# First attention of a fused two-layer kernel: q and k spread to head rows by DMA through DRAM

## The reference

```
h = ln(x); q, k, v = split(h @ w_qkv + b_qkv)            # 16 heads of 8 channels
scores = q @ k.T / sqrt(8)     # a bucket of 64 tokens sees itself (causal) and the bucket before
x1 = x + (softmax(scores) @ v) @ w_out + b_out
```

## Time and profile before

| | |
|---|---|
| time, median of 3 runs | 1061.87 us (1061.46 to 1066.82) |
| profiled execution, span | 1062.5 us |
| busy in the span: PE, DVE, ACT, POOL | 944.1, 859.6, 756.3, 405.7 us |
| granted TensorE clock, mean | 0.950 |
| first scores product of the first attention | 17.07 us |
| first instruction of the next stage | 244.5 us |

### The profile page before, as it was taken

How to read it: one execution, slowest core, us unless ns; L and a number is a source line. 1 busy time by engine, 2 the same in 40 slices (tenths; PEclk the granted TensorE clock), 3 DMA queues, 4 the chain that set the end, 5 groups by cost and what they waited for, 6 DMA issues and landing times. The chain is left out here.

```text
span 1062.5 us, 28952 instructions
## 1 busy us (share of the span) xinstructions
PE 944.1 (89%) x10222; PEld 607.5 (57%) x10222; DVE 859.6 (81%) x2328; ACT 756.3 (71%) x1476; POOL 405.7 (38%) x568
## 2 busy tenths in 40 slices
PE   5999999994889999999999999678888874899996
PEld 3788888872445444444444444246666653788862
DVE  4988988845888999868899999848888866888854
ACT  2666666645889888888888878346767653688854
POOL 3544444443354100000000000023478867676653
PEclk9999999967899999999999999969999985999998
DMA  8333333000002200032212222010111102232318
GB/s 268 123 107 107 107 106 108 24 3 20 1 6 74 72 1 1 1 104 70 77 71 75 87 66 74 20 53 22 32 52 51 54 27 74 75 86 82 85 45 221
DMA packets 61005, 72.60 MB, mean 68 GB/s; under 512 B 8875, under 2 KB 37805, under 8 KB 60865
## 3 DMA queue, kind: packets, MB, share of 16 engines
q1 hardware_dynamic: 50080, 59.36, 17.9%
q0 software_dynamic: 4544, 8.60, 2.4%
q10 hardware_dynamic: 6240, 2.79, 1.1%
HBM read 40.14 MB, written 31.49 MB: 67 GB/s over the span
## 5 line engine op out<-in xcount | busy, mean ns | idle before, releaser
L808 ACT ACTIVATE d__hf<-d__HB,dense__d 128x512 f32<-128x512 f32 x288 | 184.7, 679 | 39.2 <-PE d__HB L1047 38.2
L867 DVE TENSOR_TENSOR d__hl<-d__hf,d__hh 128x1024 f16<-128x1024 f32 x144 | 173.6, 1219 | 20.4 <-ACT d__hh L813 18.1
L813 ACT ACTIVATE d__hh<-d__hf 128x1024 f16<-128x1024 f32 x144 | 152.2, 1057 | 4.6
L781 POOL TENSOR_SCALAR d__rstd<-d__mv 128x4 f32<-128x4 f32 x16 | 14.2, 886 | 353.6 <-DVE d__mv L990 353.6
L1045 PE MATMUL d__YB<-d__hh,d__w2h 128*128 128x512 f16 x288 | 110.5, 384 | 2.5 <-DVE d__tmp L924 2.5
L1046 PE MATMUL d__HB<-d__xl,d__w1h 128*128 128x512 f16 x288 | 110.9, 385 | 0.0
L1045 PE MATMUL d__HB<-d__xh,d__w1h 128*128 128x512 f16 x288 | 110.8, 385 | 0.0
L1047 PE MATMUL d__HB<-d__xh,d__w1l 128*128 128x512 f16 x288 | 110.6, 384 | 0.0
L316 POOL TENSOR_SCALAR_AFFINE_SELECT a__pt<-a__pt 128x512 f32<-128x512 f32 x128 | 81.3, 657 | 75.4 <-ACT a__pt L364 75.3
L1046 PE MATMUL d__YB<-d__hl,d__w2h 128*128 128x512 f16 x288 | 110.1, 382 | 0.0
L1047 PE MATMUL d__YB<-d__hh,d__w2l 128*128 128x512 f16 x288 | 109.9, 382 | 0.0
(11 more groups left out here) (402 smaller groups left out, 2544.4 us busy)
## 6 DMA issues: line engine op xcount, KB each, us to landing
rows<-a__blank SPq DMA_DIRECT2D x72, 268.0 KB, 3.2
d__G<-gates SPq DMA_DIRECT2D x64, 256.0 KB, 3.2
c__xin<-rows SPq DMA_DIRECT2D x39, 134.0 KB, 2.2
dense__stage<-e_w SPq DMA_DIRECT2D x16, 256.0 KB, 3.1
b__stage<-e_w SPq DMA_DIRECT2D x32, 128.0 KB, 2.2
c__yb<-parts SPq DMA_DIRECT2D x8, 256.0 KB, 8.4
c__yb<-parts ACTq DMA_DIRECT2D x8, 256.0 KB, 8.9
out<-c__xo SPq DMA_DIRECT2D x8, 256.0 KB, 2.3
```

What stands on the lines that cost most here:

```text
L808: act.activation(hf[:, q, f], HB[:, f], gelu, scale=1.0 / WS, bias=b1[:, at:at + 1]).then_inc(s_["h_free"], 1)
L813: act.activation(hh[:, j % (LEAD + 1), f - 1:f + 1], hf[:, q, f - 1:f + 1], ACT.Copy).then_inc(s_["hi_done"], 1)
L867: dve.tensor_tensor(hl[:, p, f], hf[:, q, f], hh[:, p, f], ALU.subtract).then_inc(s_["lo%d_done" % i], 1)
```

## The change

The spread products, their evictions and the constant `spread` are gone. In their place SP writes `high` and `low` of a batch to a small DRAM buffer `spill` and, when each write has landed, reads them back six times with rows placed four apart: channel d of a head goes to rows 4d + r for r = 0, 1, 2, and the maxima's rows are now 3 and 7 (mod 32). `high` and `low` have two buffers. The rows of `qs` and `ks` that no read writes are set once at the start (VectorE: five memsets, and constants_of() behind stats(0), which also splits b_out in three). Normalising moves to ScalarE (activation with scale and bias), for which GpSimd makes -mean/sqrt(var) in two more instructions; b_out is added by one bf16 product of ones with three rows (b_out in three bf16 parts); x1 + x moves to GpSimd (`sums`). PARTS_0 is rewritten, `vproj` moves to stage 1, and SP walks the list too: x from tile 12, gate0, fetch_dense and the blanks go behind `spread` of a batch. `low` stays on VectorE.

```diff
+MAX_ROWS = (3, 7)
+SPREAD = ((0, 0, 0), (0, 1, 1), (0, 2, 0), (1, 0, 0), (1, 1, 0), (1, 2, 1))
 PARTS_0 = [
-    [("scores", 2, 0), ("vproj", 2, 0), ("shift", 3, 1), ("lift", 1, 0), ("weights", 3, 0), ("values", 4, 3),
-     ("copy", 4, 1)],
-    [("scores", 2, 1), ("mpad", 2, 0), ("qk", 1, 0), ("output", 5, 0), ("back", 4, 1), ("low", 1, 0),
-     ("weights", 3, 1), ("values", 3, 0)],
-    [("scores", 2, 2), ("proj", 1, 0), ("proj", 1, 1), ("shift", 2, 0), ("stats", 0, 0),
-     ("weights", 3, 2), ("values", 3, 1), ("copy", 3, 0)],
-    [("scores", 2, 3), ("mpad", 2, 1), ("proj", 1, 2), ("proj", 1, 3), ("back", 3, 0), ("norm", 0, 0),
-     ("weights", 3, 3), ("values", 3, 2)]]
+    [("qk", 1, 0), ("scores", 2, 0), ("low", 1, 0), ("shift", 3, 1), ("stats", 0, 0), ("weights", 3, 0), ("values", 4, 3),
+     ("copy", 4, 1), ("spread", 1, 0)],
+    [("scores", 2, 1), ("mpad", 2, 0), ("output", 5, 0), ("back", 4, 1), ("power", 0, 0), ("weights", 3, 1),
+     ("values", 3, 0)],
+    [("scores", 2, 2), ("vproj", 1, 0), ("shift", 2, 0), ("norm", 0, 0), ("weights", 3, 2), ("sums", 5, 0),
+     ("values", 3, 1), ("copy", 3, 0)],
+    [("lift", 0, 0), ("scores", 2, 3), ("mpad", 2, 1), ("back", 3, 0), ("weights", 3, 3), ("values", 3, 2)]]
...
@@ SP @@
             sp.dma_start(x[:, 4:12, :], d["x"][:, 4:12, :]).then_inc(x_mid, 16)
+            def step(what, n, k):
+                if what == "spread":
+                    wait(sp, spread_done[n % 2], READS * (n // 2))
+                    sp.wait_ge(high_done, n + 1)
+                    sp.dma_start(spill[n % 2, 0].rearrange("w p t -> p w t"), high[n % 2][:]).then_inc(spilled_high, 16)
+                    sp.wait_ge(low_done, n + 1)
+                    sp.dma_start(spill[n % 2, 1].rearrange("w p t -> p w t"), low[n % 2][:]).then_inc(spilled_low, 16)
+                    if n == 0:
+                        sp.wait_ge(preset, PRESET)
+                    wait(sp, mt_free, n * 2 - 2)
+                    wait(sp, st_full, n * 8 - 16)
+                    sp.wait_ge(spilled_high, 16 * (n + 1))
+                    for part in range(2):
+                        if part == 1:
+                            sp.wait_ge(spilled_low, 16 * (n + 1))
+                        for w, r, of in SPREAD:
+                            if of == part:
+                                dst = ks[n % 3][r::4, :, BK:BK + TB] if w else qs[n % 2][r::4, :, :]
+                                src = spill[n % 2, of, w].rearrange("(a i) t -> i a t", a=4)
+                                sp.dma_start(dst, src).then_inc(spread_done[n % 2], 16)
+                    if n == 0:
+                        sp.dma_start(x[:, 12:NT, :], d["x"][:, 12:NT, :]).then_inc(x_rest, 16)
+                        sp.dma_start(keep["gate0"][:], d["gate0"]).then_inc(gate_in, 16)
+                    if n == 1:
+                        keep["fetch_dense"](sp)
+                        sp.wait_ge(blank_set, 1)
+                    if n:
+                        for i in range(5 * n - 5, min(5 * n, BLANKS * NC_)):
+                            sp.dma_start(blanks[:, i], blank[:]).then_inc(blanked, 16)
...
@@ GpSimd @@
+                pool.tensor_scalar(mean_off[:], mv[:, :, 0], -1.0, None, ALU.mult)
...
+                pool.tensor_tensor(mean_off[:], mean_off[:], rstd[:], ALU.mult).then_inc(rstd_done, 1)
-                        ins = pool.tensor_tensor(keep["xs"][:, 2 * n + a, :], x[:, 2 * n + a, :], bo[:], ALU.add)
+                if what == "sums":
+                    pool.wait_ge(x1_done, n + 1)
+                    pool.tensor_tensor(keep["xs"][:, cut, :], keep["x1"][:, cut, :], x[:, cut, :], ALU.add)
...
@@ ScalarE @@
+                if what == "norm":
+                    wait(act, lift_full, n)
+                    act.wait_ge(rstd_done, n + 1)
+                    for a in range(2):
+                        ins = act.activation(hn[:, a, :], x[:, 2 * n + a, :], ACT.Identity, scale=rstd[:, a:a + 1],
+                                             bias=mean_off[:, a:a + 1])
-                if what == "proj":
...
@@ VectorE @@
+                for i, v in enumerate(ks):
+                    ins = dve.tensor_scalar(v[:].rearrange("p a t -> p (a t)"), v[:].rearrange("p a t -> p (a t)"),
+                                            cols[:, 5:6], None, ALU.add)
...
-                    t.inc(dve.tensor_tensor(x1, WB[:, 0:TB].rearrange("p (t c) -> p t c", t=2), xs, ALU.add))
-                    t.wait()
-                    dve.tensor_tensor(xs, x1, x[:, 2 * n:2 * n + 2, :], ALU.add).then_inc(x1_done, 1)
+                    dve.tensor_tensor(keep["x1"][:, 2 * n:2 * n + 2, :], WB[:, 0:TB].rearrange("p (t c) -> p t c", t=2),
+                                      x[:, 2 * n:2 * n + 2, :], ALU.add).then_inc(x1_done, 1)
...
@@ TensorE @@
-                if what == "proj":
...
-                        pe.matmul(dst, spread[:, 2 * w, g, :], high[:, w, :], start=True, stop=False)
-                        ins = pe.matmul(dst, spread[:, 2 * w + 1, g, :], low[:, w, :], start=False, stop=True)
@@ TensorE, scores @@
-                    pe.wait_ge(proj_free, n * 4 + 4)
+                    pe.wait_ge(spread_done[n % 2], READS * (n // 2 + 1))
@@ TensorE, output @@
+                    pe.matmul(WB[:, 0:TB], onesb[:], bparts[:].rearrange("p a c -> p (a c)"), start=False,
+                              stop=True, skip_group_check=True).then_inc(out_full, 1)
```

More of the change, by code:

```diff
@@ L167, in parts_0, with attention_0 @@
                 if what == "lift":
-                    if s > 0:
-                        step(what, s - 1, k)
+                    if s < NB + 4:
+                        step(what, s, k)
                 elif 0 <= s - stage < NB:
                     step(what, s - stage, k)
-def attention_0(nc, d, keep, rows, stages):
+def attention_0(nc, d, keep, rows, spill, stages):
     with ExitStack() as ctx:
@@ L197, in attention_0 @@
         bv = m.sb("bv", [P, 4, P])
-        high = m.sb("high", [P, 2, TB], F16)
-        low = m.sb("low", [P, 2, TB], F16)
+        high = [m.sb(f"high{p}", [P, 2, TB], F16) for p in range(2)]
+        low = [m.sb(f"low{p}", [P, 2, TB], F16) for p in range(2)]
         qs = [m.sb(f"qs{p}", [P, 4, TB], F16) for p in range(2)]
@@ L236, in attention_0 @@
         high_done = m.sem("high_done")
+        spilled_high, spilled_low = m.sem("spilled_high"), m.sem("spilled_low")
+        spread_done = [m.sem(f"spread_done{p}") for p in range(2)]
         s_full = m.sem("s_full")
@@ L279, in _ @@
+            parts_0(step)
             sp.wait_ge(blanked, 16 * BLANKS * NC_)
@@ L299, in _ @@
             pool.memset(blank[:], BLANK).then_inc(blank_set, 1)
-            pool.wait_ge(loaded, 16 * LOADS)
             def step(what, n, k):
-                if what == "stats" and n:
+                if what == "power" and n:
                     power(n)
-                if what == "norm":
-                    rows_landed(pool, n)
-                    for a in range(2):
-                        ins = pool.tensor_tensor(keep["xs"][:, 2 * n + a, :], x[:, 2 * n + a, :], bo[:], ALU.add)
-                    ins.then_inc(xb_done, 1)
+                if what == "sums":
+                    pool.wait_ge(x1_done, n + 1)
+                    cut = slice(2 * n, 2 * n + 2)
+                    pool.tensor_tensor(keep["xs"][:, cut, :], keep["x1"][:, cut, :], x[:, cut, :], ALU.add)
                 if what == "weights":
@@ L398, in step @@
                     dve.bn_aggr(mv[:, 1, :], st[:, 1, :]).then_inc(var_done, 1)
[L399 to L406 removed]
+                    if n == 0:
+                        constants_of()
                 if what == "low":
                     dve.wait_ge(high_done, n + 1)
+                    wait(dve, spilled_low, 16 * (n - 1))
                     for a in range(2):
[L410 to L411 removed]
+                        ins = dve.scalar_tensor_tensor(out=low[n % 2][:, a, :], in0=WA[:, a * TB:(a + 1) * TB],
+                                                       scalar=cols[:, 2 + a:3 + a], in1=high[n % 2][:, a, :],
                                                        op0=ALU.add, op1=ALU.subtract)
@@ L473, in step @@
                     wait(pe, lift_free, n)
[L474 removed]
+                    wait(pe, low_done, min(n, NB))
                     if n < NB:
@@ L2291, in constants @@
     c["bits"] = np.ascontiguousarray(np.broadcast_to(steps.reshape(1, 45).view(np.float32), (P, 45)))
-    c["spread"] = np.stack([heads_to_rows(c["ident16"], 4, r) for r in ((0, 1), (2,), (0, 2), (1,))], 1)
     low = np.zeros((P, 2), np.float32)
@@ L2310, in layout @@
     c = constants()
-    out = {"ident": c["ident"], "kpad": c["kpad"], "ident16": c["ident16"]}
+    out = {"ident": c["ident"]}
     out["x"] = a["L0_attn_x"]
```

143 lines of the change are left out of this document (64 added, 79 removed).

## The result

The changed kernel takes **1057.35 us** at the median of 5 runs (1055.60 to 1061.23), the kernel before in the same comparison 1061.87 (5 runs). The ratio is 0.9937, with an interval of 0.991 to 0.9964: faster by 0.6%, where 14.6 us (1.4%) were forecast. The profiled execution took 1061.23 us, its span is 1059.5 us at a mean granted clock of 0.935; the profile of before has 1062.5 us at 0.950.

What follows compares the result with a forecast made beforehand. The prediction took TensorE to bound the kernel at 13.42 us a step. Twelve steps at 12.13 gain 15.5 us and the start loses 0.9: -14.6, so 1047 us at the median, range 1036 to 1064.

Steps and rivals of the forecast that it cites:

- The steady step: First attention, full steps: 13.42 us falls to 12.1, set by hand-overs between VectorE and TensorE; chance 0.45.
- the chain that was walked: Within a step: VectorE's work from first reduction to back(4,1), 6.43 us, which TensorE awaits before shift(2,0).
- The start: Before the 12 steps: first scores 3 us later, three steps win back 0.7 each, so 0.9 us late.
- The transfers: SP's spill writes and reads in steady steps: 3.7 us of cover, so they cost nothing.
- rival D: Steady steps set by two transfers in a row: step 15.0 us with late landings, 1084 us; chance 0.13.
- The norm: Normalising moved to ScalarE: about 1.3 us off VectorE per step, hidden on ScalarE before lift asks for it.
- The casts: VectorE's mpad casts beside GpSimd's selects: 206 ns as a rule, up to 722; step 11.8 to some 12.5 us.
- rival C: Steady steps: GpSimd's new work slides selects onto mpad and delays values; 12.8 us, 1055 us; chance 0.18.
- The stages after: Stages behind the first attention: no term in the sum, so nothing gained or lost.
- The drain: Last four steps of the first attention: 0 gained or lost.
- B: Steady steps: TensorE alone sets 11.5 us, reductions being early enough; 1040 us; chance 0.21.
- E: Steady steps: TensorE waits for transfers and its clock falls to 1.2 GHz; 17.3 us, 1112 us; chance 0.03.

Runs made afterwards that it cites:

- e6: The changed kernel with its blanks issued in the dense stage and the LayerNorm statistics of batches 1 to 15 left out; 1053.32 us in one run.
- e1: The changed kernel with products on idle data added in TensorE's gaps of the first two batches; 1056.97 us, ratio 0.9964 to before.
- e2: The changed kernel with x from tile 12 behind batch 2, dense weights behind 4, six blanks a batch from batch 3; 1072.0 us, ratio 1.0065 to before.
- e3: The changed kernel with the edits of e1 and e2 together; 1069.71 us, ratio 1.0046 to before.
- e5: The changed kernel with all 72 blanks issued in the dense stage, eleven behind each pair of expert weights; 1059.82 us, ratio 0.9984 to before.
- e12: As e11, with products on idle data added in TensorE's gaps of the first two batches; 1047.44 us, ratio 0.9862 to before.
- e11: As e10, with x from tile 12 and the gate behind batch 1 and the dense weights behind batch 4; 1052.78 us, ratio 0.9906 to before.
- e10: The changed kernel with all 72 blanks in a row behind the dense stage's last load of weights; 1051.26 us, ratio 0.9889 to before.
- e7: As e5, with x from tile 12 behind batch 1, dense weights behind 6, bias parts behind batch 2's statistics; 1059.47 us, ratio 0.9978 to before.
- e4: The changed kernel with the LayerNorm statistics of batches 1 to 15 left out; 1060.76 us in one run.
- e8: The kernel before with only the norm moved to ScalarE, plus its two GpSimd instructions; 1067.32 us, ratio 1.0047 to before.
- e9: The changed kernel with the norm put back on VectorE; 1100.22 us, ratio 1.0359 to before.

## Why the prediction was wrong, point by point

The profiled executions give the account of the first attention: start 9.85 us late, 12 steps from 61.78 to 207.63 in 145.85 us instead of 161.07, so 15.2 won, and the drain 33.3 us instead of 35.8, 2.5 won: 7.9 us sooner. Forecast were 0.9 late, 15.5 won, 0 in the drain. Of the 14.6 us forecast the two profiled executions show 3.0: 8.95 went in the start, 0.3 in the steps and 4.9 in the later stages, and 2.5 came in the drain.

- **The steady step: right, 12.11 for 12.1, but not by the chain that was walked.** `shift(2,0)` did not wait for `back(4,1)`, which was done 0.56 us before it; TensorE lost its 0.6 us in small pieces behind reductions and `output`, and without the statistics the step fell to 11.5. The walked chain counted the casts of `mpad` at their mean of before; with the 0.20 and 0.23 us measured, its own sum is 11.8. That 12.1 was hit is luck. That VectorE sets it holds, and 11.5 as TensorE's own was right to 0.02 us (e6).
- **The start: the step that failed.** "I let them win back 0.7 us each", so that "the 12 steps start 0.9 us late", took half of the steady gain for steps that lost instead: they started 9.85 us late. Of these, 3.71 stand there at batch 0 (20.78 for 17.07), 1.48 come in the step to batch 1, 4.75 in the step to batch 2 and nothing in the third. The 3.7 are near the 3 forecast, in part by luck: the terms named there (1.8 saved, 6 to 7 for transfers, 0.5 to 1 for VectorE) add up to 4.7 to 6.2.
- **The start, step by step.** Lengths in us from one batch's first scores to the next:

| | before | changed | e1 | e2 | e3 | e5 | e12 |
|---|---|---|---|---|---|---|---|
| batch 0 to 1 | 10.88 | 12.36 | 12.37 | 10.30 | 12.32 | 12.47 | 12.08 |
| batch 1 to 2 | 11.76 | 16.51 | 15.63 | 16.73 | 12.01 | 13.86 | 12.01 |
| batch 2 to 3 | 12.22 | 12.13 | 14.98 | 12.13 | 15.24 | 11.80 | 11.80 |

  The step to batch 1 waits for rows behind the moved loads; without them it takes 10.30 (e2) or 10.80 (e11), and the low clock cost nothing to be seen there (12.45 at 0.99 in e5 and e10, 12.36 at 0.60 in the changed kernel). The step to batch 2 has both costs at once, and each hides the other: late rows (moved loads and five blanks ahead of its spill) and TensorE at 1.2 GHz (e1 to e3). The prediction priced neither: of the loads it said "their readers are steps away", which looks at who reads them and not at what is queued behind them, and the low clock it had only for steady steps. e5 and e10 (no blanks ahead) took 13.86 and 13.84 us for that step, but their low stretch was also shorter within it, 9.9 us for 12.1, so the 2.7 us less aren't the blanks' alone; the full clock took off 1.8 to 2.2 more (12.01 in e12, 11.68 in e7). e12, with all of it, has batch 3 at 55.78, 6.0 us back; its three steps take 35.9 us where before's took 34.86. The shortest seen of each (10.30 in e2, 11.68 in e7, 11.80 in e10) would make 33.8, 1.1 us won where 2.1 were forecast, and no run has all three. Why the clock fell at 16 to 22 us in some versions and only at 33 to 36 in others stays open.
- **The transfers.** Read issues took 0.60 to 0.63 us, not 0.45; the write of `high` landed after 3.3 us, not 1.8 (`low` 2.2). So the cover was 1.5 to 2 us for 3.7, and SP issued for 7.8 us of a step (0.49 + 0.38 + 3.69 + 3.23), not 5.9, and waited 2.5 more for `low` and for landings. The DMA engines were at 0.52, not at "about 0.45". "I cost the transfers at nothing in steady steps" still held from batch 3 on, except at the last batch, whose step lacks its `qk`: 1.81 us. e2 and e4 show how near rival D was.
- **The norm** hides on ScalarE as said (0.87 us a pair). Alone in the old order it costs 0.4 us a step, by e8's rows through its two instructions on GpSimd; in the new order GpSimd has room for them. For VectorE it was worth more than its work: e9 loses 3.1 us a step, not the 1.3 counted, since it stands last before `lift`, and the clock fell too.
- **The casts** stood clear of the selects (0.20 and 0.23), so rival C did not come. In e9 they took up to 0.66 and 0.59 us, and the norm's two tensor_scalar 0.78 and 0.70 beside a select. The rule of the Trainium skill, SBUF — State Buffer, section "Who interferes with whom", that a cast or tensor_scalar in a two-port mode and a GpSimd instruction block each other for a whole instruction, fits e9's trace: a tensor_scalar that started 0.07 us behind a select took 0.68 us (111.47), the one just before it 0.34. In the changed kernel it cost nothing.
- **The stages after.** The sum put them at nothing; they took 4.9 us more than in before. 1.6 of them lie in the dense stage. From its last large product to the end it is 392.1 us in before, 395.4 after, 395.8 in e10 and 392.6 in e12, and TensorE was granted 1.2 GHz for 65, 77, 77 and 66 us of that. The length goes with the clock; what decides in a run how long it is low was not found and stays open.
- **The drain**, put at 0, gave 2.5 us. TensorE was granted 1.2 GHz for 19 us of it in before and for 12 after; no run tests whether that is the cause.

Rivals: B was TensorE's own bound and came only with the statistics left out (e6, and three steps of e4); D was the nearest; the low clock of E came not in the steady steps but in the start, where the prediction had no place for it. The time itself lies within the range, close to C's 1055, but not by C's mechanism.

## What to carry to other kernels

When a chain of products is replaced by a chain of transfers, price the start apart: there the latency is bare, the queue's other loads stand in it, and TensorE can be at 1.2 GHz just when it has to catch up (37.5 to 51.2 us here). Where one step may have two limits, take away each and then both: here either alone gave less than 1 us of 16.51, and both 4.5. Walk the issuing queue like an engine, with what stands behind each moved load, and give large writes with no hurry (here 20 MB of blanks) to a stretch in which that queue and the DMA engines are idle. And test the parts of a change both ways: one part alone cost 5 us here, and leaving it out of the change left a kernel 36 us slower than before.

## What the runs showed of the hardware

- A read of 64 KB from DRAM into every fourth of 128 partitions keeps SP 0.60 us at the median, a write of 128 KB 0.38, a blank of 268 KB 0.48.
- A write of 128 KB landed after 1.8 to 4.7 us in the first attention, where the DMA engines were half busy (0.52); in the profile of before the one write of that size landed in 1.8.
- TensorE was busy for 13.84 of 13.84 us in e10's step from 33.29 and was granted 0.64 of its clock in it (1.2 GHz from 33.0 to 43.2), after a wait of 1.81 us; e12, with some more products in TensorE's gaps, had 1.00 in the same step. So TensorE can stay at 1.2 GHz for 10 us while it is busy without a gap.
- A tensor_scalar of VectorE (128x128, f32) took 0.34 us alone and up to 0.78 beside a select of GpSimd.
